# Eight places instead of four for the gathered token rows of a mixture-of-experts loop

## The reference

```python
logits = x_flat @ gate_w.T
top_v, top_i = jax.lax.top_k(logits, K)              # K = 2 of E = 8 experts
probs = jax.nn.softmax(top_v.astype(jnp.float32), axis=-1).astype(logits.dtype)
...
hidden = jax.nn.silu(x_flat @ wge.T) * (x_flat @ wue.T)    # 512 wide
return (acc + we[:, None] * (hidden @ wde.T), None)
...
x = x + 0.5 * _L0_ffn_ref(_layernorm(x, axis=-1), ...)
x = x + _L0_attn_ref(_layernorm(x, axis=-1), ...)
x = x + 0.5 * _L0_ffn_ref(_layernorm(x, axis=-1), ...)
```

## Time and profile before

| what | value |
|---|---|
| time, median of three runs | 2813.0 us (2808.58 to 2814.91) |
| span of the profiled execution | 2637.8 us |
| the median less that span | 175.2 us (an own run time of the profiled execution is not listed) |
| busy over the span: PE, DVE, POOL, ACT | 85%, 85%, 83%, 72% |
| expert stage 1, first gather to last scatter | 104.34 to 494.63 us |
| expert stage 2, first gather to last scatter | 2203.30 to 2592.82 us |
| gathers (L484), 284 in both stages | 297.1 us busy, 1046 ns mean |
| scatters (L494), 284 in both stages | 287.7 us busy, 1013 ns mean |
| mean granted clock of TensorE | 0.956 of full speed |

### The profile page before, as it was taken

One profiled execution on the slowest core, in us unless ns is written; L12 is line 12 of the kernel. 1 busy time (PEld: TensorE's weight loads), 2 busy tenths in 40 slices (PEclk: granted clock), 3 DMA queues, 4 the chain that ended last, 5 costly groups with the idle time before them and its releaser, 6 DMA issues.

```text
span 2637.8 us, 49017 instructions
## 1 busy us (share of the span) xinstructions
PE 2244.2 (85%) x15840; PEld 1920.7 (73%) x15840; DVE 2254.8 (85%) x3430; ACT 1909.6 (72%) x3628; POOL 2198.0 (83%) x1402
## 2 busy tenths in 40 slices
PE   4899999768888898898898898988988768999992
PEld 3799999547676677777777676766777647999982
DVE  8766666789999999999999999999999897666666
ACT  4355555378998998998999899999898544555551
POOL 3577777369999999999999999999999936777771
PEclk8899999889999999999999999999999878999996
DMA  7011111433333333333333333333333240111116
GB/s 247 17 48 50 49 49 49 121 107 104 105 109 106 109 102 101 106 107 100 109 103 102 110 103 105 110 106 106 105 102 111 76 160 25 49 50 49 49 50 204
DMA packets 156813, 248.60 MB, mean 94 GB/s; under 512 B 22082, under 2 KB 66018, under 8 KB 155874
## 3 DMA queue, kind: packets, MB, share of 16 engines
q1 hardware_dynamic: 137568, 202.79, 25.9%
q0 software_dynamic: 18208, 37.26, 5.2%
q10 hardware_dynamic: 866, 6.43, 0.6%
HBM read 213.10 MB, written 33.29 MB: 93 GB/s over the span
## 4 chain that ended last, share of the span: by engine, by line
POOL 28%; PE 23%; issue 22%; DVE 14%; ACT 8%; DMA 4%; POOLq 0%; ACTq 0%; DVEq 0%; SPq 0%
POOL buf L484 10%; POOL buf L545 9%; DVE buf L914 6%; PE bank L1544 6%; POOL token_outputs L494 5%; PE bank L1419 4%; DMA buf<-state_rows 3%; PE bank L1329 3%; PE bank L1519 3%; POOL buf L532 2%; DVE buf L901 2%; ACT scaled L1194 2%; ACT over L1161 2%; DVE bank L886 2%; PE bank L1348 2%
## 5 line engine op out<-in xcount | busy, mean ns | idle before, releaser
L545 POOL TENSOR_TENSOR buf<-buf 128x1024 f32<-128x1024 f32 x512 | 1199.9, 2378 | 33.8 <-PE bank L1544 28.9
L914 DVE TENSOR_TENSOR_SCAN buf<-over,bank 128x512 f32<-128x512 f32 x832 | 953.6, 1198 | 5.2 <-PE bank L1519 2.6
L1161 ACT ACTIVATE over<-wgu,negA 128x510 f32<-128x510 f32 x832 | 541.2, 710 | 39.6 <-DVE buf L914 28.5
L1544 PE MATMUL bank<-id_sb,buf 128*128 128x128 f32 x4096 | 521.8, 282 | 6.3 <-POOL buf L545 6.3
L1544 PEld LDWEIGHTS bank<-id_sb,buf 128*128 128x128 f32 x4096 | 483.9, 146 | 55.8 <-issue 46.5
L1348 PE MATMUL bank<-parts 128*128 128x256 f32 x3408 | 480.3, 291 | 3.3 <-DVE buf L764 1.9
L1348 PEld LDWEIGHTS bank<-parts 128*128 128x128 f32 x3408 | 428.8, 192 | 7.2 <-issue 4.1
L1194 ACT ACTIVATE scaled<-wd_sb,I 128x256 f32<-128x256 f32 x896 | 377.3, 498 | 22.3 <-PE bank L1519 22.2
L494 POOL DMA_INDIRECT token_outputs<-buf,slot_out x284 | 287.7, 1013 | 111.1 <-issue 83.2
L484 POOL DMA_INDIRECT buf<-token_rows,slot_token x284 | 297.1, 1046 | 95.4 <-issue 89.7
L1519 PE MATMUL bank<-id_sb,scaled 128*128 128x128 f32 x1792 | 257.2, 281 | 91.3 <-ACT scaled L1194 40.8
(11 more groups left out here) (170 smaller groups left out, 2978.0 us busy)
## 6 DMA issues: line engine op xcount, KB each, us to landing
buf<-state_rows SPq DMA_DIRECT2D x608, 256.0 KB, 3.2
token_rows<-buf SPq DMA_DIRECT2D x32, 256.0 KB, 2.3
wd_sb<-token_outputs SPq DMA_DIRECT2D x16, 512.0 KB, 4.1
buf<-token_outputs SPq DMA_DIRECT2D x16, 512.0 KB, 4.9
buf<-token_rows,slot_token POOLq DMA_INDIRECT x284, 2.6
token_outputs<-buf,slot_out POOLq DMA_INDIRECT x284, 2.3
out<-X SPq DMA_DIRECT2D x16, 256.0 KB, 3.8
wgu<-wgT ACTq DMA_DIRECT2D x1, 2048.0 KB, 8.1
```

Source lines behind the costliest of these rows:

```text
L545: pool.tensor_tensor(hC[:, b, :].rearrange("p (c w) -> p c w", c=C), hs[:, b, :].rearrange("p (c w) -> p c w", c=C), Cs[:, b, :].unsqueeze ...
L914: V.tensor_tensor_scan(hs[:, b, w], dA[:, b, c, :, :].rearrange("p s t -> p (s t)"), source, 0.0, ALU.mult, ALU.add).then_inc(s[f"scan_don ...
L1161: ins = A.activation(dA[:, n % R, c, :, 1:], delta[r][:, c * W:(c + 1) * W].rearrange("p (s t) -> p s t", s=S)[:, :, 1:], ACT.Exp, scale=n ...
L1544: ins = M.matmul(bank[4 + q // 2][:, at:at + P], hC[:, n % R, c * W + q * P:c * W + (q + 1) * P], id_sb[:, :], is_transpose=True, start=Fa ...
```

## The change

xin gets eight places (X_BUFS = 8). POOL gathers tiles 0 to 7 first, and then for each i tile i + 8 and the scatter of tile i; its wait for turned_pe follows. The eight places need 2048 columns and lie at column 8192 of buf, in the part from which the token rows were stored to DRAM in the routing stage (rowsN, columns 6656 to 10751). PE's written-out beginning has eight tiles, its loop eight per trip over tiles 8 to 63 (7 trips), its end seven tiles. The loops of DVE and ACT stay at four tiles per trip, and yo and wd_e at four places.

```diff
--- before.py
+++ after.py
@@ -63,6 +63,7 @@
 
 ACT_TILES = 2
 ROW_BUFS = 8
+X_BUFS = 8
 CHUNKS = (0, 1, 4, 8, 12, 16)
 
 
@@ -148,7 +149,9 @@
     TILES = (2 * T + E * (TP - 1)) // TP
     LOOPS, LAST = TILES // 4, TILES % 4
     USES = [len(range(b, TILES, 4)) for b in range(4)]
-    assert LAST
+    X_USES = [len(range(b, TILES, X_BUFS)) for b in range(X_BUFS)]
+    X_LOOPS, X_LAST = TILES // X_BUFS, TILES % X_BUFS
+    assert LAST and X_LAST
     assert D == P and C == 2 and I == 512 and W == 512 and NG == NP and NG % 2 == 0
     CONV, CB, DTB, DSK, ALOG = 0, 4, 5, 6, 7
 
@@ -226,7 +229,7 @@
             return buf[:, at:at + n]
 
 
-        xin = carve(0, 4 * HT * D).rearrange("p (b h d) -> p b h d", h=HT, d=D)
+        xin = carve(8192, X_BUFS * HT * D).rearrange("p (b h d) -> p b h d", h=HT, d=D)
         x_hi = parts[:, 0:2 * TP].rearrange("p (b d) -> p b d", d=TP)
         x_lo = parts[:, 2 * TP:4 * TP].rearrange("p (b d) -> p b d", d=TP)
         w_hi = parts[:, 4 * TP:4 * TP + 4 * I].rearrange("p (b w) -> p b w", w=2 * I)
@@ -308,7 +311,7 @@
             hot_pe hot_part is_col hot_pool hot_act ids_ready
             gate_spread shift_all_done xn_act lT_pe lT_act lback_pe stats_done dve_norm act_norm xt_pre rstd_done xn_done moment before_done xt_done xnT_done
             logit_done logits_act route_dve route_pe route_act xin0 xin1 xin2
-            xin3 st0 st1 st2 st3 turned_pe xhi_act xlo_dve whi_act wlo_dve gate_pe up_pe
+            xin3 xin4 xin5 xin6 xin7 st0 st1 st2 st3 turned_pe xhi_act xlo_dve whi_act wlo_dve gate_pe up_pe
             silu_act hid_dve down_pe yo_act comb_done comb_first stored diff_done mask_done slots_done
             experts_done expA_done dtp_zeroed diag_ready taps_spread taps_ready parts_ready skip_ready gT_pe gT_done BT_pe BT_done duT_pe duT_done scaled_done turned0 turned1 gated du_done dve_pre
             act_pre pe_pre vareps_pre rstd_pre shift_pre res_done pe_post negA_done bcB_ready bc_copied bc_stored C_in0 C_in1 C_in2 C_in3 B_in0 B_in1 dA_ready
@@ -478,13 +481,13 @@
 
                 def get_tokens(i):
 
-                    wait(pool, s["turned_pe"], m * TILES + i - 3)
+                    wait(pool, s["turned_pe"], m * TILES + i + 1 - X_BUFS)
                     pool.sem_inc(s["out_turn"], 1)
                     for h in range(HT):
                         pool.indirect_dma_start(
-                            out=xin[:, i % 4, h, :], out_offset=None, in_=xn_rows[:, :],
+                            out=xin[:, i % X_BUFS, h, :], out_offset=None, in_=xn_rows[:, :],
                             in_offset=bass.IndirectOffsetOnAxis(ap=slot_token[:, i * HT + h:i * HT + h + 1], axis=0)
-                        ).then_inc(s[f"xin{i % 4}"], DMA)
+                        ).then_inc(s[f"xin{i % X_BUFS}"], DMA)
 
                 def put_outputs(i):
 
@@ -499,11 +502,11 @@
                 for b in range(ROW_BUFS):
                     pool.wait_ge(s[f"xn_stored{b}"], (m + 1) * NG // ROW_BUFS * DMA)
                 pool.wait_ge(s["ids_ready"], m + 1)
-                for i in range(4):
+                for i in range(X_BUFS):
                     get_tokens(i)
                 for i in range(TILES):
-                    if i + 4 < TILES:
-                        get_tokens(i + 4)
+                    if i + X_BUFS < TILES:
+                        get_tokens(i + X_BUFS)
                     put_outputs(i)
 
             moe(0)
@@ -1334,7 +1337,7 @@
                 pe.wait_ge(s["loaded_w"], (3 + 3 * m) * DMA)
 
                 def turn_slots(i, q, k):
-                    pe.wait_ge(s[f"xin{q}"], (m * USES[q] + k + 1) * HT * DMA)
+                    pe.wait_ge(s[f"xin{q}"], (m * X_USES[q] + k + 1) * HT * DMA)
                     wait(pe, s["xlo_dve"], m * TILES + i)
                     for h in range(HT):
                         ins = M.transpose(bank[6][:, h * P:(h + 1) * P], xin[:, q, h, 0:D], id_sb[:, :])
@@ -1371,11 +1374,11 @@
                                            wd_e[:, q, c * D:(c + 1) * D], start=(c == 0), stop=(c == IC - 1))
                     ins.then_inc(s["down_pe"], 1)
 
-                def four(k, count=4):
+                def eight(k, count=X_BUFS):
                     for q in range(count):
-                        i = k * 4 + q
+                        i = k * X_BUFS + q
                         if not (isinstance(i, int) and i == TILES - 1):
-                            turn_slots(i + 1, (q + 1) % 4, k + 1 if q == 3 else k)
+                            turn_slots(i + 1, (q + 1) % X_BUFS, k + 1 if q == X_BUFS - 1 else k)
                         gate(i, q % 2, 0)
                         up(i, q % 2, 0)
                         if not (isinstance(i, int) and i == 0):
@@ -1384,10 +1387,10 @@
                         up(i, q % 2, 1)
 
                 turn_slots(0, 0, 0)
-                four(0)
-                with pe.Fori(1, LOOPS) as k:
-                    four(k)
-                four(LOOPS, LAST)
+                eight(0)
+                with pe.Fori(1, X_LOOPS) as k:
+                    eight(k)
+                eight(X_LOOPS, X_LAST)
                 down(TILES - 1, (TILES - 1) % 2, LAST - 1)
 
             moe(0)
```

## The result

| | median of 20 runs, us | range |
|---|---|---|
| kernel before | 2813.94 | 2808.58 to 2821.03 |
| changed kernel | 2821.24 | 2816.29 to 2826.67 |

The ratio is 1.0027, 95% interval [1.002, 1.0033]: 7.3 us slower, where 23 us faster was forecast. On four other chips the same kernel before takes 2637 to 2639 us, and there the changed kernel is faster (0.9964 [0.995, 0.9977] and 0.9955 [0.9938, 0.9971] on two of them). Both halves of this need explaining: why the sign differs, and why the gain, where there is one, is half of what was forecast.

What follows compares the result with a forecast made beforehand. POOL's four indirect DMAs per tile were taken as the bound; 127.5 + 18 x 5.53 + 44 x 5.28 plus the tail gave 11.5 us less per stage, 23.0 together, so 2813.0 - 23.0 = 2790 us, range 2776 to 2806.

Steps and rivals of the forecast that it cites:

- Around the span the runs take 175.2 us more: Outside the profiled span: 2813.0 us timed against 2637.8 profiled, the difference taken as untouched by the change.
- rival A: Locked expert loop: DVE's copy falls at a bad place in POOL's cycle, 2800 to 2823 us, 2820 if clear; chance 0.07.
- Start: Stage start: 18 gathers instead of 10 fill POOL's 6.72 us idle; first scatter at 127.5 instead of 123.50.
- PE's loop of eight: PE's doubled loop body: instruction reloading taken as 0, bounded by say 3 us per branch back, six branches per stage.
- the address: New xin places in buf: the stage's first gather already waits for the token-row stores there, so cost 0.
- the wait on turned_pe: POOL's wait before a gather: keeps its distance to PE's transposes, so cost 0.
- Free run: Expert loop up to tile 18: PE no longer starves, keeps 4.86 us per tile; POOL pays 5.53.
- Lock on yo: From tile 22 ACT's copy_out waits for the scatter four tiles earlier, so POOL sets PE's pace again.
- Cycle of 5.28: POOL's locked cycle per tile: 5.16 us plus 0.12 for DVE's copy 0.80 us into the second scatter; bounds 5.16, 5.66.
- B: Expert loop: PE becomes the bound through its doubled loop body and a slower clock, 2844 us; chance 0.04.
- D: Locked expert loop: DVE's copy falls into POOL's gaps, 10.6 us more gain, 2779 us; chance 0.15.
- E: Both stages: POOL bounds both kernels and loses its start gain in the longer free run, 2808 to 2815 us; chance 0.07.

Runs made afterwards that it cites:

- b_small: Kernel before plus 320 small DMAs on SP beside the first expert stage, on a chip with long tiles: 2855.41 against 2816.42 us, ratio 1.0141.
- loop8: Kernel before with only PE's loop changed to eight tiles per trip, four places and four gathers ahead kept: ratio 1.0001.
- place8192: Kernel before with its four xin places moved to column 8192 of buf: ratio 1.0001.
- a_again: Changed kernel, unaltered, run again on a quiet chip: 2627.92 us against 2637.26 for the kernel before, ratio 0.9964.
- a_pieces: Changed kernel with DVE's two low_w subtractions of 128x512 cut into eight of 128x128, on a quiet chip: 2621.07 us, ratio 0.9942.

## Why the prediction was wrong

**The step that failed** is "Around the span the runs take 175.2 us more (2813.0 against 2637.8, a median against one profiled execution), which the change leaves alone". Around a span lie 2.1 us (2638.76 and 2636.7; 2820.24 and 2818.1). The other 173 us are in the two expert stages of the timed runs: on a chip where before takes 2816, b_small's second stage takes 475.7 us where the profiled one took 389.5, twice 86. So the loop that was timed was another one than the loop that was read, and what POOL saves is not on its path: in the changed kernel's trace POOL waits 86.5 us before 31 scatters between 150 and 540 us, for ACT, and ACT for PE. The gap of 175 us was the sign that the profile didn't stand for the runs, and it was put aside as a constant.

**What replaces it.** On such a chip PE's signals arrive late in the expert loop, and PE stops inside series of matmuls that wait for nothing. That is where the 18 gathers hurt: they hold ACT up by 5.8 us at the third tile, and the fourth turn comes 8 to 13 us late. It is a rival that the prediction didn't have. The gain at the start that it did have, POOL's 6.72 us filled, buys nothing when the loop behind is paced by PE: POOL even stands 4.30 us before its first scatter. That 2821 lies next to the 2820 of rival A is chance; A's dear phase of POOL's cycle is not what happened in that run, where POOL is not the bound.

**Step by step, on a quiet chip, where the argument can be held against its own kind of run:**

- *Start.* 18 gathers, no idle time, first scatter at 128.05 (forecast 127.5): right.
- *PE's loop of eight, the address, the wait on turned_pe*: 0, right (loop8, place8192; of the idle time before a_again's gathers the profile puts 1.2 us to PE's turns).
- *Free run* at 5.53 until tile 18: 5.56 until tile 16, right.
- *Lock on yo*: right, ACT waits for the scatter 49 times, 123.0 us in the first stage, from tile 18 on instead of 22; the copy 0.83 us into the scatter.
- *Cycle of 5.28*: wrong in size, 5.43 in the first stage. Four tiles take 5.34, 5.34, 5.41 and 5.64; the forecast had one phase where there are four, which repeat with the four tiles of ACT's and DVE's loop body (that their branches shift the phase was not tested). 46 tiles x 0.15 = 6.9 us, most of the 8.4 us by which the last scatter (491.46) missed 483.1. The cause of the price was wrong as well: it is the subtractions, which were running when the gather of 304.53 started, and not the copy 0.81 us into it. That 0.13 was near at all is luck, since the copy keeps a fixed distance from the subtractions; the price measured in the first stage is 5.43 - 5.16 = 0.27.
- *Sum.* Stages of 387.3 and 381.2 us against 390.3 and 389.5: 11.3 us, measured 9.3 and 11.9, forecast 23.0. In the second stage the fourth tile of each round falls free (5.16 instead of 5.64), which is why it gained more.
- *Rival A* (the dear phase) came about half way: 0.27 us per tile, between the 0.12 of the forecast and the 0.38 from which A decides. B, D and E didn't occur.

**What is open.** Why two of the six chips of the experiments, and the one of the comparison, deliver PE's signals late. What the traces show: the records of the signals are incomplete in the expert stages there (23,641 in the changed kernel's trace against 29,796 in a_again, and 5,904 of the missing ones are of landings; the stretch from one expert stage to the next has all of its own); the transfers are hardly slower (POOL's queue moves 15.28 MB in 7456 packets at 14.8% of 16 engines in 390 us there, 14.40 MB in 7016 packets at 17.0% in 300 us here: 0.124 and 0.116 us per packet); PE doesn't wait for its instructions (three packets of q8 between 150 and 540 us, none in b_small between 2385 and 2740); more small landings make it worse (b_small: 39 us); and it ends with the gathers, the last of which starts at 543.69: the last tiles take 4.9 us again:

```profile
553.87 0.38 PE L1343 MATMUL bank<-id_sb,buf 128*128 128x128 f32 x2
...
558.74 0.38 PE L1343 MATMUL bank<-id_sb,buf 128*128 128x128 f32 x2
```

All this fits something that has to carry signals or their records and is full while gathers and scatters both land; which of the two it is, no run tells. The Trainium skill, "NOTIFIC — the notification-queue block", section 7.1 (Overflow), says that records can be dropped or can stall the engine that produces them. If it were that, runs without records would not have the long tiles; no run here shows it. Why the change loses only 7.3 us in the comparison, where one pair of stages gives 6.1 for one of the two, was not settled; the trace of the kernel before is from another chip.

No kernel here beats both everywhere. On quiet chips a_pieces is the fastest that computes all of the reference (0.9942), not clearly apart from the changed kernel; on a chip with long tiles it was not run.

## What to carry to other kernels

Compare a profile's span with the times it is to explain before reading anything in it: a gap of 6% is not a constant to add back but a sign that another loop was timed. Work that is moved ahead of a loop adds its own traffic there, and a place that the profile shows as idle is free only for what it doesn't disturb. Before an operation is blamed for a neighbour's longer one, look for what ran when that one *started*; here a copy that always follows two subtractions carried their phase.

## What the hardware did that was not expected

- A GpSimd gather or scatter that starts while DVE subtracts two SBUF tiles of 128x512 ends 0.81 to 0.91 us after that subtraction's end (136 of 137 in a_again): 1.24 us with 0.4 us left, 1.46 with 0.6, against 0.99; one that started 0.11 us before the subtraction took 0.98. The copy of 128x512 from SBUF to SBUF does the same when it is already running (1.24 with 0.38 left). Without those subtractions the kernel takes 2594.85 instead of 2627.92 us.
- The same kernel takes 2636.5 to 2639.3 us on four chips and 2794 and 2816 on two others, the runs on one chip within 0.4% of each other. The difference lies in the two expert stages: between them, from 584.38 to 2291.43, the changed kernel took 1707.1 us where a_again took 1707.6.
- 320 DMAs of 8 KB beside one stage cost 38 and 39 us on the latter two.
- On those chips TensorE's signals came up to 6.1 us after the matmul that gives them, ScalarE's and VectorE's within 0.02 us; on a quiet chip TensorE's too.
